# An 8-expert gated layer on rows sorted by expert, and two layer norms in one pass

## The chip, the core and the metric

The kernel runs on one core of one Trainium2 chip. It is one launch. The metric is the device time of that launch in microseconds, median over runs. The engines are TensorE (PE, its weight loads are PEld), VectorE (DVE), ScalarE (ACT), GpSimd (POOL) and the queue of SyncE (SP), which issues most DMAs; GpSimd issues the indirect ones, whose row numbers come from a table in on-chip memory.

## What is computed

Eight residual layers on x, four sequences of 512 tokens with 128 features: four times an attention and then a feed-forward layer, each on the layer norm of x and scaled by the tanh of a gate. The change touches two of them, the third attention (over latents) and the third feed-forward layer:

```
# third attention: its queries come from the norm of a norm
x = x + tanh(g_xattn[2]) * attn(ctx_1024, layernorm(x), ...)
  # inside: xn = ln(ctx) * g + b;  ln = ln(latents) * g' + b'

# third feed-forward: T = 2048 tokens, D = 128, F = 352, E = 8, TOP_K = 2
scores = softmax(xt @ router_w)
expert_weights, expert_idx = top_k(scores, 2)
h = gelu(xt @ w1[e]) * (xt @ v1[e])          # for every e
y = h @ w2[e]
out = sum over the two chosen e of weight * y  +  bias
x = x + tanh(g_ffn[2]) * out
```

The reference computes all eight experts for each token and keeps two.

## The kernel before

x is held transposed on chip (`c.xT`, features on the 128 partitions, 2048 tokens along the row), its layer norm in `c.xn`. The stages follow one another; each is one or several blocks, and between two blocks all engines meet at a barrier.

A layer norm (`layer_norm`) takes a list of pieces of at most 512 columns. For each piece TensorE multiplies by a centring matrix, ScalarE squares, TensorE averages the squares, ScalarE takes the logarithm of variance plus eps and the exponential of minus a half of it, VectorE multiplies. The third attention (`perceiver_attention`) calls it twice in two blocks: `norm_x` writes the norm of x to `c.xn` (4 pieces), and a second call norms `c.xn` once more in place (4 pieces) and the context (1 piece of 308 columns).

The third feed-forward layer (`dense_glu_moe`) starts with `norm_x` and `route`, which gives each token its two best experts (`top`, `place`). `expert_weights` spreads them over a table of eight weights per token, on VectorE. The main block is a loop over the 4 sequences; in each it goes through 24 units, three blocks of hidden features (128, 128 and 96) for each of 8 experts, in an order written by hand: `HP` and `VP` (hidden features on the partitions, 512 tokens along the row), then `YP` of the unit before, four products of 128 tokens. ScalarE takes the gelu (`gl`), VectorE multiplies it by `VP` (`hv`) and adds the finished expert, weighted, into `acc`. At the end of a sequence `acc` is turned back, scaled, and added to x. All 8 experts are computed for all tokens.

An earlier stage, the second feed-forward layer (`capacity_moe`, 64 experts, 3 per token), already works on sorted rows, and its rows in the trace are the nearest there are for the new code. It ranks tokens by matrix products with a triangular matrix, makes two tables of row numbers (`slot_in`, `slot_out`), and runs 32 pairs of experts. Each pair fetches 128 rows by an indirect DMA (`xs`), turns them (`XT`), multiplies (`HN`), turns the result (`HP`), multiplies again (`YP`), and scatters 128 rows to DRAM by another indirect DMA. At the end all rows are read back (`yg`), weighted (`acc`), turned and added to x.

## Time and profile before

| | |
|---|---|
| device time, median of 3 runs | 1845.82 us (1844.06 to 1846.3) |
| the profiled execution, device time | 1841.34 us |
| its span in the trace | 1839.5 us |
| mean granted clock of TensorE | 0.917 of full speed |
| PE busy | 1565.9 us, 85% |
| DVE, ACT, POOL busy | 847.9, 762.3, 432.8 us |

The profile is one execution, 4.5 us below the median of the runs. A busy TensorE row is not the same as TensorE at its peak, since matmuls overlap and their ends are modelled. In the rows further down, a stretch from A to B is in microseconds from the span's start, and PEclk is the clock that was granted to TensorE, 1.00 for 2.4 GHz and 0.50 for 1.2 GHz. The trace shortens tile names: `f_` stands for any feed-forward layer, so `f_W` is one of the weights W1 and W2, and `a_nx`, `a_nl` are the two norms of the third attention.

### The profile page before, as it was taken

The page shows a single profiled execution, that of the slowest core. Times are in us where ns is not written, and L with a number is a line of the kernel's source. Part 1 is how long each engine was busy: PE and PEld are TensorE (multiplying, and loading weights), DVE is VectorE, ACT ScalarE, POOL GpSimd, SP SyncE. Part 2 cuts the span into 40 slices and gives each one's busy share as a digit, 9 for nine tenths or more (in the row PEclk, how much of TensorE's full clock was granted, in tenths as well). Part 3 has the DMA queues.
Part 4 walks back from the last instruction along what each step waited for, and adds up shares of the span by engine and source line. Part 5 has one row for each costly group of instructions (what it writes and reads, how often), then busy time and mean ns, then how long its engine had stood idle before and what let it go on. Part 6 is the DMA issues. An engine that isn't in the chain of part 4 may idle for free. (4 is left out here: it accounts for less than half of the span.)

```text
span 1839.5 us, 21220 instructions
## 1 busy us (share of the span) xinstructions
PE 1565.9 (85%) x7428; PEld 694.9 (38%) x7428; DVE 847.9 (46%) x1637; ACT 762.3 (41%) x1379; POOL 432.8 (24%) x386
## 2 busy tenths in 40 slices
PE   6857778639946999999999999977999998776997
PEld 2223332325523333333333333324565564123443
DVE  5842278443333555455545545524343334524343
ACT  3443345334434656565655655541222224342111
POOL 1000062026401455455545445420000000100000
PEclk9978889759956999999999999997999999887999
DMA  8200030529240000000000000020000000000000
GB/s 279 92 12 0 26 81 1 191 80 345 100 122 1 1 1 1 1 1 1 1 1 1 1 0 1 1 98 1 1 0 0 0 0 29 1 30 27 0 0 23
DMA packets 32494, 71.27 MB, mean 39 GB/s; under 512 B 5747, under 2 KB 19827, under 8 KB 31375
## 3 DMA queue, kind: packets, MB, share of 16 engines
q1 hardware_dynamic: 30358, 65.93, 10.4%
q0 software_dynamic: 2048, 4.20, 0.8%
q8 instruction: 51, 0.84, 0.2%
q14 instruction: 37, 0.30, 0.1%
HBM read 65.92 MB, written 7.34 MB: 40 GB/s over the span
## 5 line engine op out<-in xcount | busy, mean ns | idle before, releaser
L1762 DVE TENSOR_REDUCE a_nmp<-a_SP 128x2 bf16<-128x590 f32 (+1 forms) x256 | 197.0, 769 | 267.5 <-PE a_SP L1531 265.6
L1690 ACT ACTIVATE a_prob<-a_TP 128x512 f32<-128x512 f32 x256 | 138.9, 595 | 154.8 <-PE a_TP L1519 153.7
L1549 PE MATMUL a_O<-a_prob,a_V 128*64 128x512 f32 (+1 forms) x640 | 172.2, 617 | 1.5 <-DVE a_on L1800 1.5
L1516 PE MATMUL a_TP<-a_qn,a_kn 64*128 64x512 f32 (+1 forms) x640 | 166.3, 597 | 1.0 <-DVE a_negm L1825 0.5
L1847 POOL TENSOR_TENSOR a_acc<-a_acc,a_prob 128x512 f32<-128x512 f32 x128 | 158.7, 1271 | 2.3 <-DVE a_acc L1813 1.6
L1245 DVE TENSOR_TENSOR f_hv<-f_gl,f_VP 128x512 f32<-128x512 f32 (+1 forms) x96 | 65.8, 686 | 163.5 <-ACT f_gl L1211 163.5
L1211 ACT ACTIVATE f_gl<-f_HP 128x512 f32<-128x512 f32 (+1 forms) x96 | 57.2, 595 | 200.7 <-PE f_VP L1193 200.7
L1837 POOL TENSOR_TENSOR a_acc<-a_prob 128x512 f32<-128x512 f32 x64 | 79.8, 1266 | 205.1 <-ACT a_prob L1690 205.1
L818 POOL TENSOR_TENSOR a_kxb<-a_kT,hmu 128x1232 bf16<-128x1232 f32 x9 | 21.7, 2409 | 414.4 <-DVE a_kxb L606 367.7
L1180 PEld LDWEIGHTS f_YP<-f_W,f_hv 128*128 128x128 f32 (+1 forms) x768 | 100.5, 192 | 47.9 <-issue 44.3
L1191 PE MATMUL f_HP<-xn,f_W 128*128 (+1 forms) x192 | 104.1, 625 | 16.4 <-PEq L1095 11.0
L1180 PE MATMUL f_YP<-f_W,f_hv 128*128 128x128 f32 (+1 forms) x768 | 101.7, 275 | 2.0 <-DVE f_hv L1245 2.0
L1193 PE MATMUL f_VP<-xn,f_V 128*128 (+1 forms) x192 | 101.7, 612 | 0.0
L665 DVE TENSOR_REDUCE a_nm<-a_SP 128x6 bf16<-128x462 f32 x144 | 78.3, 579 | 39.9 <-PE a_SP L365 24.4
L1531 PEld LDWEIGHTS a_SP<-a_knb,a_qnb 64*128 64x128 bf16 x512 | 24.8, 93 | 163.3 <-issue 86.7
L1531 PE MATMUL a_SP<-a_knb,a_qnb 64*128 64x295 bf16 (+1 forms) x512 | 76.5, 295 | 3.2 <-DVE a_nmp L1762 2.6
L827 POOL TENSOR_TENSOR a_biasQk<-a_biasQ,a_negQ 128x1232 bf16<-128x1232 f32 x12 | 32.4, 2710 | 198.1 <-DVE a_negQ L723 180.7
L1359 ACT ACTIVATE f_sl<-f_GP 128x512 f32<-128x512 f32 x40 | 23.9, 597 | 116.5 <-PE f_BP L1346 100.6
L1366 DVE TENSOR_TENSOR f_hu<-f_sl,f_UP 128x512 f32<-128x512 f32 x40 | 27.5, 688 | 81.3 <-ACT f_sl L1359 81.3
L365 PE MATMUL a_SP<-a_kxb,a_qb 128*128 128x462 bf16 x144 | 50.6, 374 | 15.3 <-DVE a_nm L665 9.7
L1519 PE MATMUL a_TP<-a_negm,a_sel 64*128 64x512 bf16 (+1 forms) x320 | 60.8, 376 | 0.0
L1516 PEld LDWEIGHTS a_TP<-a_qn,a_kn 64*128 64x128 f32 (+1 forms) x640 | 48.4, 181 | 30.0 <-DVE a_negm L1825 23.4
(377 smaller groups left out, 2776.6 us busy)
## 6 DMA issues: line engine op xcount, KB each, us to landing
ring_w<-in_F_w SPq DMA_DIRECT2D x64, 512.0 KB, 8.3
f_yg<-dispatched SPq DMA_DIRECT2D x12, 256.0 KB, 5.3
a_maskT<-in_maskT SPq DMA_DIRECT2D x4, 576.0 KB
a_biasT<-in_biasT SPq DMA_DIRECT2D x1, 2304.0 KB
f_b<-in_F_b SPq DMA_DIRECT2D x1, 1664.0 KB, 8.5
f_W<-in_F_w SPq DMA_DIRECT2D x1, 1536.0 KB, 11.9
f_W<-in_F_w SPq DMA_DIRECT2D x1, 1408.0 KB, 6.2
f_V<-in_F_v SPq DMA_DIRECT2D x1, 1408.0 KB, 9.1
```

What stands on the lines that cost most here:

```text
L665: nc.vector.tensor_reduce(nm[:, b % 2, qt, :].rearrange("p (g h) -> p g h", g=QUAD)[:, qs, hs], SP[:, slot_of[("unit", k)] % 2, 0:hi - lo] ...
L1180: mm = nc.tensor.matmul(YP[:, e % 2, q * P:(q + 1) * P], hv[0:wide(j), u % 3, q * P:(q + 1) * P], W2[0:wide(j), u, :], start=(j == 0 and q ...
L1191: nc.tensor.matmul(HP[0:wide(j), u % 2, :], W1[:, at:at + wide(j)], c.xn[:, tokens(b)], start=True, stop=True)
L1193: nc.tensor.matmul(VP[0:wide(j), u % 2, :], V1[:, at:at + wide(j)], c.xn[:, tokens(b)], start=True, stop=True).then_inc(hv_ready, 1)
L1245: nc.vector.tensor_tensor(hv[0:f, u % 3, :], gl[0:f, u % 2, :], VP[0:f, u % 2, :], ALU.mult).then_inc(multiplied, 1)
L1516: nc.tensor.matmul(TP[0:hi - lo, h, :], kn[HALF[h], g % 4, lo:hi], qn[HALF[h], g % 4, :], start=True, stop=False)
L1531: mm = nc.tensor.matmul(SP[:, h, 0:hi - lo], qnb[HALF[h], g % 2, q * P:(q + 1) * P], knb[HALF[h], g % 2, lo:hi], start=True, stop=True)
L1549: mm = nc.tensor.matmul(O[HALF[h], :], V[0:n, g % 4, kc, HALF[h]], prob[0:n, kc, h, :], start=kc == 0, stop=kc == NC - 1)
L1690: nc.scalar.activation(prob[0:n, kc, h, :], TP[0:n, h, :], ACT.Exp, bias=rowneg[0:n, g // NP:g // NP + 1] if kc == 0 else 0.0)\
L1762: nc.vector.tensor_reduce(nmp[:, u // 2, u % 2, :], SP[:, :, 0:hi - lo], AX.X, ALU.max, negate=True).then_inc(s_used, 1)
L1837: nc.gpsimd.tensor_tensor(acc[:, g % 2, h, :], prob[:, 1, h, :], prob[:, 2, h, :], ALU.add).then_inc(summed, 1)
L1847: nc.gpsimd.tensor_tensor(acc[:, g % 2, h, :], acc[:, g % 2, h, :], prob[:, kc, h, :], ALU.add).then_inc(summed, 1)
```

## The change

**Norms.** The third attention calls `layer_norm` once, with the context first and then the four pieces of x, reading `c.xT`. For the norm of a norm it uses that the variance of the first result is known: pieces named in `twice` take the logarithm of (1 + eps) times the variance plus eps squared.

**Experts.** `expert_weights` and the loop over all experts go. Each token now makes two rows, one for each chosen expert, and the 4096 rows are sorted by expert; every expert's part is filled up to a multiple of 128, so there are at most 39 tiles of 128 rows, each of one expert. A new block makes the tables on VectorE and TensorE and writes the normed rows to DRAM. The main block is written out for the 39 tiles, with one indirect fetch and one indirect scatter for each on GpSimd, and with the products the other way round: tokens on the partitions, 352 hidden features along the row, so that `hv` has to be turned (`HT`) before the last product. Which columns of W1, V1 and W2 a tile uses is read into a register of TensorE (`value_load`). The bias is added to x by one VectorE instruction at the start of the block. The end is the code of the second feed-forward layer, now the function `add_rows`, with two rows per token in place of three.

Diff, cut to its core:

```diff
@@ layer_norm
-                    nc.scalar.activation(lnv[:, i % 2, :w], var[:, i % 4, :w], ACT.Ln, bias=eps).then_inc(logged, 1)
+                    grow, add = (1.0 + eps, eps * eps) if i in twice else (1.0, eps)
+                    nc.scalar.activation(lnv[:, i % 2, :w], var[:, i % 4, :w], ACT.Ln, bias=add,
+                                         scale=grow).then_inc(logged, 1)
@@ perceiver_attention
-        norm_x(c, name + "_nx", start_loads)
-        layer_norm(c, name + "_nl", [(c.xn[:, s:s + S], c.xn[:, s:s + S], S) for s in range(0, T, S)]
-                   + [(c.ctxrep[:, :, 0:SK], cn[:, :], B * SK)])
+        layer_norm(c, name + "_n", [(c.ctxrep[:, :, 0:SK], cn[:, :], B * SK)]
+                   + [(c.xT[:, s:s + S], c.xn[:, s:s + S], S) for s in range(0, T, S)], start_loads, twice=(1, 2, 3, 4))
@@ dense_glu_moe, the table block (VectorE, for each of the two choices k)
+                    for k in range(TOPK):
+                        step(nc.vector.tensor_tensor(prod[:, :, :], hot[:, k, :, :], at[:, :, :], ALU.mult))
+                        step(nc.vector.tensor_reduce(pos[:, k, :], prod[:, :, :], AX.X, ALU.add))
+                        step(nc.vector.tensor_tensor(hit[:, k, :, :], per_tile(pos[:, k, :], HITS),
+                                                     over_tiles(bounds[:, :], HITS), ALU.is_ge))
+                        nc.vector.tensor_tensor(ids[:, k, :, 0:NT], hit[:, k, :, 0:NT], hit[:, k, :, 1:HITS],
+                                                ALU.subtract).then_inc(chosen, 1)
+                        step(nc.vector.tensor_reduce(full[:, k, :], hit[:, k, :, 1:HITS], AX.X, ALU.add))
...
+                        nc.vector.tensor_tensor(ranks[:, k, :, :], over_tiles(lanes[:, :], P),
+                                                per_tile(within[:, k, :], P), ALU.is_equal).then_inc(ranked, 1)
...
+                @block.gpsimd
+                def _(pool):
+                    for g in range(G):
+                        pool.wait_ge(stored[g], 16)
+                    pool.wait_ge(slot_in_made, 1)
+                    for n in range(FIRST):
+                        fetch(n)
@@ dense_glu_moe, the main block (FIRST = 2, XR = 8, YR = BEHIND = 4, WARM = 4, NT = 39)
+                for n in range(FIRST, XR):
+                    fetch(n)
+                for n in range(NT):
+                    if n + XR < NT:
+                        pool.wait_ge(rows_turned, n + 1)
+                        fetch(n + XR)
+                    if n >= BEHIND:
+                        scatter(n - BEHIND)
...
+                def up(n):
+                    pe.wait_ge(buf_ready, n + 1)
+                    if n >= 2:
+                        pe.wait_ge(multiplied, n - 1)
+                    columns = bass.ds(expert[n] * F, F)
+                    nc.tensor.matmul(HP[:, n % 2, 0:F], bufT[:, n % BR, :], W1[:, columns], start=True,
+                                     stop=True).then_inc(h_ready, 1)
+                    nc.tensor.matmul(VP[:, n % 2, 0:F], bufT[:, n % BR, :], V1[:, columns], start=True,
+                                     stop=True).then_inc(v_ready, 1)
+
+                def hidden(n):
+                    pe.wait_ge(multiplied, n + 1)
+                    if n:
+                        pe.wait_ge(h_copied, n)
+                    for j in range(NJ):
+                        mm = nc.tensor.transpose(HT[0:wide(j), j * P:(j + 1) * P], hv[:, n % 2, j * P:j * P + wide(j)],
+                                                 c.ident[:, :])
+                    mm.then_inc(h_turned, 1)
+
+                def down(n):
+                    pe.wait_ge(h_copied, n + 1)
+                    if n:
+                        pe.wait_ge(y_kept, n)
+                    for j in range(NJ):
+                        mm = nc.tensor.matmul(YP[:, 0:D], hT[0:wide(j), n % 2, j, :],
+                                              W2[0:wide(j), bass.ds(expert[n] * (NJ * P) + j * P, P)],
+                                              start=(j == 0), stop=(j == NJ - 1))
+                    mm.then_inc(y_ready, 1)
...
+                expert[0] = pe.value_load(expert_of[0:1, 0:1], min_val=0, max_val=E - 1)
+                for _ in range(WARM):
+                    nc.tensor.matmul(HP[:, 1, :], c.center[:, :], c.xn[:, 0:512], start=True, stop=True)
+                turn(0)
+                turn(1)
+                for n in range(NT):
+                    up(n)
+                    if n + 1 < NT:
+                        expert[n + 1] = pe.value_load(expert_of[0:1, n + 1:n + 2], min_val=0, max_val=E - 1)
+                    if n + 2 < NT:
+                        turn(n + 2)
+                    if n:
+                        hidden(n - 1)
+                    if n >= 2:
+                        down(n - 2)
...
+                for n in range(NT):
+                    act.wait_ge(h_ready, n + 1)
+                    if n >= 2:
+                        act.wait_ge(multiplied, n - 1)
+                    nc.scalar.activation(gl[:, n % 2, :], HP[:, n % 2, 0:F], ACT.Gelu).then_inc(gelued, 1)
+                    if n + 2 < NT:
+                        evacuate(n + 2)
+                    if n:
+                        copy_hidden(n - 1)
```

TensorE in the main block before, from the start of a sequence: `HP` and `VP` are products of 512 tokens with a block of W1 or V1, `YP` stands for four products of 128 tokens.

```order
L1191 MATMUL f2_HP<-xn,f2_W1 128x512
L1193 MATMUL f2_VP<-xn,f2_V1 128x512
L1178 ISA
L1180 MATMUL f2_YP<-f2_W2,f2_hv 128x128 x4
L1191 MATMUL f2_HP<-xn,f2_W1 96x512
L1193 MATMUL f2_VP<-xn,f2_V1 96x512
L1178 REGISTER_ALU
L1180 MATMUL f2_YP<-f2_W2,f2_hv 128x128 x4
```

TensorE in the main block now, one tile: `XT` turns the rows of the tile after next, `HT` turns the hidden rows of the tile before, `YP` is the last product of the tile before that.

```order
L1478 MATMUL f2_HP<-f2_W1,f2_bufT 128x352
L1480 REGISTER_ALU
L1480 MATMUL f2_VP<-f2_V1,f2_bufT 128x352
L1512 TENSOR_LOAD f2_expert_of
L1512 ISA x2
L1471 MATMUL f2_XT<-ident,f2_xs 128x128
L1488 MATMUL f2_HT<-ident,f2_hv 128x128
L1488 MATMUL f2_HT<-ident,f2_hv 128x128
L1488 MATMUL f2_HT<-ident,f2_hv 96x128
L1497 ISA
L1497 MATMUL f2_YP<-f2_W2,f2_hT 128x128
L1497 ISA
```

Three `YP` products stand in each tile. A load of a register with two instructions that check it stands between the last big product and the transposes, and instructions that compute an address stand before the products that use it.

VectorE between the router and the main block before, where `f2r_hot` marks the chosen experts:

```order
L1106 MEMSET f2r_wt 128x2048
L1114 TENSOR_TENSOR f2r_hot<-iota,f2r_place 128x128
L1116 TENSOR_TENSOR f2r_hot<-f2r_hot,f2r_top 128x128
L1114 TENSOR_TENSOR f2r_hot<-iota,f2r_place 128x128
L1116 TENSOR_TENSOR f2r_hot<-f2r_hot,f2r_top 128x128
L1117 TENSOR_TENSOR f2r_wt<-f2r_hot 128x16x8
```

The same place now, from the second choice on, where `f2_ids` and `f2_ranks` are the operands of the products `IX` that give the tables (the first of these rows up to `f2_ids<-f2_ids,iota` stand for the first choice as well):

```order
L1336 TENSOR_TENSOR f2_prod<-f2_hot,f2_at 128x128
L1337 TENSOR_REDUCE f2_pos<-f2_prod 128x16
L1338 TENSOR_TENSOR f2_hit<-f2_pos,f2_bounds 128x640
L1340 TENSOR_TENSOR f2_ids<-f2_hit 128x16x39
L1342 TENSOR_REDUCE f2_full<-f2_hit 128x16
L1343 SCALAR_TENSOR_TENSOR f2_within<-f2_full,f2_pos 128x16
L1345 TENSOR_TENSOR f2_ranks<-f2_lanes,f2_within 128x2048
L1348 TENSOR_TENSOR f2_ids<-f2_ids,iota 128x16x39
L1350 TENSOR_TENSOR f2_begun<-iota,f2_base 128x312
L1353 TENSOR_REDUCE f2_te<-f2_begun 128x39
L1354 TENSOR_SCALAR f2_te<-f2_te 128x39
L1355 CAST f2_expert_of<-f2_te 128x39
```

VectorE's part between router and main block grows from 6 instructions to 52. GpSimd, which had nothing in this stage, gets 78 indirect DMAs.

## Rows read from the trace of the kernel before

**Rows 1.** Stretches: busy time of each engine (instructions), PEclk, DMA share, GB/s.
```profile
1251.00:1255.30 4.30, 0.01 (x1) 0.01 (x1) 3.38 (x8) 0.37 (x1) 0.00 (x0) 0.50 0.00 0
1255.30:1534.70 279.40, 264.10 (x1168) 161.63 (x1169) 102.79 (x232) 61.19 (x102) 0.00 (x0) 0.96 0.00 0
364.80:403.60 38.80, 10.20 (x144) 8.87 (x144) 22.68 (x45) 16.91 (x61) 7.76 (x8) 0.50 0.17 44
403.60:503.90 100.30, 98.39 (x810) 54.25 (x810) 31.15 (x99) 42.21 (x97) 52.80 (x55) 0.98 0.61 224
503.90:532.30 28.40, 4.46 (x16) 2.87 (x16) 11.51 (x37) 5.12 (x16) 1.70 (x2) 0.55 0.44 118
532.30:545.30 13.00, 9.90 (x16) 3.78 (x16) 2.77 (x4) 8.29 (x14) 0.00 (x0) 0.76 0.52 184
545.30:559.50 14.20, 11.28 (x20) 4.68 (x20) 3.24 (x5) 9.34 (x17) 0.00 (x0) 0.80 0.00 1
```

**Rows 2.** Timeline, one unit of the all-expert loop: start, us, engine, line, operation.
```profile
1382.16 1.02 PE L1193 MATMUL f_VP<-xn,f_V 128*128 x2
...
1383.02 1.06 PE L1180 MATMUL f_YP<-f_W,f_hv 96*128 96x128 f32 x8
...
1383.22 0.60 ACT L1211 ACTIVATE f_gl<-f_HP 128x512 f32<-128x512 f32 x1 [2.02 <-PE f_VP L1193]
...
1383.85 0.69 DVE L1245 TENSOR_TENSOR f_hv<-f_gl,f_VP 128x512 f32<-128x512 f32 x1 [1.93 <-ACT f_gl L1211]
...
1383.91 1.02 PE L1191 MATMUL f_HP<-xn,f_W 128*128 x2
```

**Rows 3.** Timeline, one pair in the second feed-forward layer's loop.
```profile
450.03 1.08 PE L2155 MATMUL f_HN<-ring_w,f_bufT 128*64 128x512 f32 x4
...
451.04 0.33 PE L2147 MATMUL f_XT<-ident,f_xs 128*128 128x128 f32 x1
...
451.30 1.09 PE L2175 MATMUL f_YP<-ring_w,f_hg 128*64 128x128 f32 x16
...
451.37 0.98 POOL L2125 DMA_INDIRECT dispatched<-f_ys,f_slot_out  x1 [0.62 <-DVE f_ys L2216]
...
452.33 0.66 PE L2164 MATMUL f_HP<-ident,f_hn 128*128 128x128 f32 x4
...
452.66 0.97 POOL L1945 DMA_INDIRECT f_xs<-token_rows,f_slot_in  x1 [0.30 <-issue]
...
452.91 1.08 PE L2155 MATMUL f_HN<-ring_w,f_bufT 128*64 128x512 f32 x4
```

**Rows 4.** Timeline, making of the tables and start of the loops.
```profile
1252.85 0.29 DVE L1114 TENSOR_TENSOR f2r_hot<-iota,f2r_place 128x128 f32<-128x128 f32 x1
...
378.95 1.22 DVE L2014 TENSOR_TENSOR f_ranks<-iota,f_pos 128x1024 bf16<-128x1024 f32 x1
...
390.44 0.18 DVE L2024 CAST f_slot_in<-f_row 128x32 uint32<-128x32 f32 x1
...
391.51 1.15 POOL L1945 DMA_INDIRECT f_xs<-token_rows,f_slot_in  x1 [93.93 <-DVE f_slot_in L2024]
...
400.47 0.94 POOL L1945 DMA_INDIRECT f_xs<-token_rows,f_slot_in  x1 [0.30 <-issue]
...
403.67 6.56 PE L2182 MATMUL f_HP<-xn,center 128*128 128x512 f32 x10 [14.57 <-PEq L1970]
...
410.78 1.08 PE L2155 MATMUL f_HN<-ring_w,f_bufT 128*64 128x512 f32 x4 [0.34 <-ACT f_bufT L2242]
```

**Rows 5.** Timeline, the end of the second feed-forward layer.
```profile
503.77 0.29 DVE L2216 TENSOR_TENSOR f_ys<-f_YP,f_b 128x128 f32<-128x128 f32 x1 [1.29 <-PE f_YP L2175]
...
504.93 0.97 POOL L2125 DMA_INDIRECT dispatched<-f_ys,f_slot_out  x1 [0.30 <-issue]
...
512.30 9.01 SPq L2277 DMA_DIRECT2D f_yg<-dispatched  x12
...
518.18 2.20 DVE L2306 SCALAR_TENSOR_TENSOR f_acc<-f_yg,f_gk,f_acc 128x128 f32<-128x128 f32 x8 [14.11 <-ACT f_acc L2286]
```

More of the change, by code:

```diff
@@ L127, in _, with layer_norm @@
             dve.wait_ge(got, 8)
-def layer_norm(c, name, pieces, loads=None, scratch=None, eps=LN_EPS):
+def layer_norm(c, name, pieces, loads=None, scratch=None, eps=LN_EPS, twice=()):
     nc = c.nc
@@ L1123, in dense_glu_moe @@
     nc, d = c.nc, c.dram
-    E, F = 8, 352
+    E, F, TOPK, G = 8, 352, 2, 4
     NJ = -(-F // P)
-    U = E * NJ
-    with ExitStack() as ctx, c.phase():
+    NT = (T * TOPK + E * (P - 1)) // P
+    HITS, PAD = NT + 1, 8
+    XR, BR, YR, BEHIND, FIRST, WARM = 8, 4, 4, 4, 2, 4
+    ROWS_AT = 5120
+    xrows = nc.dram_tensor("glu_rows", [T, D], F32, kind="Internal").ap()
+    with ExitStack() as whole, ExitStack() as ctx, c.phase():
+        gk = whole.enter_context(nc.sbuf_tensor(name + "_gk", [P, TOPK, TILES], F32))
         router = Router(c, ctx, name + "r", E, "F2_router")
@@ L1145, in dense_glu_moe @@
[L1145 to L1151 removed]
         def wide(j):
             return min(P, F - j * P)
+        W1, V1 = sb("W1", [P, E * F]), sb("V1", [P, E * F])
@@ new lines, in dense_glu_moe, with _, scatter @@
+        h_turned, h_part, h_copied, y_ready, y_kept, bias_made, biased = (
+            sem(n) for n in ("h_turned", "h_part", "h_copied", "y_ready", "y_kept", "bias_made", "biased"))
+        scattered = [sem(f"scattered{i}") for i in range(YR)]
+        with nc.Block() as block:
+            @block.gpsimd
+            def _(pool):
+                def scatter(n):
+                    pool.wait_ge(y_kept, n + 1)
+                    nc.gpsimd.indirect_dma_start(
+                        out=c.disp[:, :], out_offset=bass.IndirectOffsetOnAxis(ap=slot_out[:, n:n + 1], axis=0),
+                        in_=ys[:, n % YR, :], in_offset=None).then_inc(scattered[n % YR], 16)
+                for n in range(FIRST, XR):
[6 more added lines that the diff above has]
+                        scatter(n - BEHIND)
+                for n in range(NT - BEHIND, NT):
+                    scatter(n)
+                for i in range(YR):
+                    pool.wait_ge(scattered[i], 16 * len(range(i, NT, YR)))
@@ L1216, in _, with keep @@
+                copy_hidden(NT - 1)
+                act.wait_ge(h_part, NT)
             @block.vector
             def _(dve):
-                dve.wait_ge(loaded, 64)
+                def keep(n):
+                    dve.wait_ge(y_ready, n + 1)
+                    if n >= YR:
+                        dve.wait_ge(scattered[n % YR], 16 * (n // YR))
+                    nc.vector.tensor_copy(ys[:, n % YR, :], YP[:, 0:D]).then_inc(y_kept, 1)
+                dve.wait_ge(w_loaded, 64)
                 nc.vector.tensor_tensor(bias[:, 1:2], bias[:, 0:1], c.gates[:, gate:gate + 1],
@@ L1253, in _ @@
-                dve.wait_ge(x_updated, B)
+                dve.wait_ge(bias_made, 1)
+                nc.vector.tensor_scalar(c.xT[:, :], c.xT[:, :], bias[:, 1:2], None, ALU.add).then_inc(biased, 1)
+                for n in range(NT):
+                    dve.wait_ge(gelued, n + 1)
+                    dve.wait_ge(v_ready, n + 1)
+                    if n >= 2:
+                        dve.wait_ge(h_turned, n - 1)
+                    nc.vector.tensor_tensor(hv[:, n % 2, :], gl[:, n % 2, :], VP[:, n % 2, 0:F],
+                                            ALU.mult).then_inc(multiplied, 1)
+                    if n >= 2:
+                        keep(n - 2)
@@ L1256, in shared_moe @@
+                keep(NT - 2)
+                keep(NT - 1)
+                dve.wait_ge(biased, 1)
+        ctx.close()
+        add_rows(c, name, gate, ROWS_AT, TOPK, gk)
 def shared_moe(c, name, gate):
@@ L2326, in flamingo_kernel @@
+        add_rows(c, name, gate, 4096, TOPK, gk)
 def flamingo_kernel(nc, dram, out):
```

414 lines of the change are left out of this document (270 added, 144 removed).

## The prediction

> **What bounds the kernel now.** First the page's busy shares: TensorE is the busiest engine by far, so a stage is worth what TensorE's row in it is worth. Then the busy time by stretches [rows 1]. The loop over all experts takes 279.4 us, and TensorE is busy for 264.1 of them at a granted clock of 0.96. It is bound by its matmuls. Then the timeline of one unit [rows 2]: `VP` starts at 1382.16, `YP` at 1383.02 and the next `HP` at 1383.91, with no gap between them, while ScalarE and VectorE work 0.60 and 0.69 us of each 2.6. For the new code I read the second feed-forward layer, which has the same kind of loop: its tables take 38.8 us, its loop 100.3 us with TensorE busy for 98.4, its end 28.4 us [rows 1]. Last the two norms of the third attention, 13.0 and 14.2 us [rows 1].
>
> **The main loop: the price of a tile.** From rows 2, a product of 512 columns takes 0.86 us and eight passes of 128 columns 0.89 with the change to the next product, 0.107 a pass (a product in f32 is two passes). So `HP` and `VP` of 352 columns cost 2 x 0.86 x 352/512 = 1.18 us. The three last products are six passes of 128 columns, 0.65. Four transposes (one of fetched rows, three of `hv`) cost 0.58, as the four do between 452.33 and 452.91 [rows 3]. Changing kind costs something: in rows 3 the parts alone would be 0.86 + 0.14 + 0.86 + 0.58 = 2.44, and a pair takes 452.91 - 450.03 = 2.88, so 0.44 for three changes, 0.15 each. Here there are two such changes and one like the 0.03 of rows 2. Sum 1.18 + 0.65 + 0.58 + 0.33 = 2.74 us.
>
> Who else could pace a tile? GpSimd: a scatter starts at 451.37 and the fetch behind it at 452.66 [rows 3], 1.29 us, 1.27 without the difference of the two, so one of each is 2.56 us. That is below 2.74, but close. ScalarE: a gelu and three copies, none over the 0.60 of rows 2, under 2.0 us. VectorE: a product of 352 columns (0.53, between the 0.29 for 128 and the 0.69 for 512) and a copy (0.29). The buffers: `HT`, `YP` and `XT` are single. `copy_hidden(n-1)` ends about 2.7 us into tile n (up 1.18, turn and three transposes to 1.9, two copies), and the next transposes need it at 2.74 + 1.5. `keep` is done 0.5 us into the next tile and is needed at 1.9. No wait ends last there.
>
> **The register load** is what the trace of before doesn't show. Its lower bound is 0: the last wait ahead of it that comes late is for `y_kept`, 0.5 us into the tile before, and what is queued by then and behind it (three transposes' rest, the last products, the next `HP` and `VP`) keeps TensorE busy until 2.74 + 1.18 = 3.9 us. A load of up to 2 us is covered, if the sequencer may run that far ahead. The upper bound is that the load starts only when the products have ended, so nothing covers it. The nearest row is another engine that picks up a fresh number and starts: from `slot_in` written at 390.62 to GpSimd's first DMA at 391.51, 0.89 us [rows 4]. With the check and the address instructions I put the upper end at 1.2 us. I take 0 in the loop, because the wait ahead of it ends early enough, and 1.0 once at the start, where nothing covers it.
> The Trainium skill (DMA: Bandwidth & Descriptors, section Latency and other measured facts) gives a floor of about 600 ns for a `tensor_load`; no row here shows one. Uncovered in each of 39 tiles it would be an estimate of 23 us, and the forecast would be 1740. The same skill (TensorE: Matmul & The Clock Gate, section Architectural detail: the array is 16× 32×32, not 1× 128×128) says that TensorE's queue is 64 deep, by which the load would be covered; rows 2 agree as far as they go, since `YP` follows `VP` without a gap though a wait stands between them.
>
> **The tables.** VectorE's instructions cost 0.16 us plus 1.04 ns per element of a row: 0.29 for 128, 1.22 for 1024 [rows 4]. Ahead of the two choices stand 20 small ones, 4.9 us, with some 14 waits on the one before at 0.035, together 5.4. Each choice has 128, 128, 640, 624, 624, 16, 2048 and 624 elements: 0.29 + 0.29 + 0.83 + 0.81 + 0.81 + 0.18 + 2.29 + 0.81 = 6.3, with waits 6.5, twice 13.0. The experts of the tiles cost 1.5 (312 elements twice, two small ones). The products `IX` of the second choice run beside these. Then four instructions to `slot_in`, 1.2. Sum 21.1 us. From the start of the `slot_in` instruction to the first warming product it is 403.67 - 390.44 = 13.23 us with eight fetches [rows 4]; six fetches fewer at (400.47 - 391.51)/7 = 1.28 leave 5.5. Together 21.1 - 0.2 + 5.5 = 26.4 us from the start of the block at 1251.0. From there to the first `up` 410.78 - 403.67 = 7.1 [rows 4], less one warming product (0.86), plus the first load (1.0): 7.3. The other six fetches and the addition of the bias (2048 elements, 2.3 us on VectorE) lie beside the warming. If the table block's rates are off by a fifth, it is 4 us either way.
>
> **The end.** From the start of the last `up` the chain is: products 1.18, `hv` to 1.9, the transposes queue behind the tile before to 3.3, two copies to 4.25, last product to 5.0, `keep` to 5.5 us. What follows is the 28.4 us of the layer before (503.9 to 532.3, rows 1), with these differences: the last row is kept at 504.06 there (-0.15), and two scatters stand behind it, one here (-0.6, the last one starts at 504.93, rows 5). Twelve reads are issued in 9.01 us [rows 5], eight in 6.0 (-3.0), and the last group has four additions in place of eight at 2.20 us (-1.1). That leaves 23.5.
>
> **The sum for this stage.** After 1251.0: 26.4 + 7.3 + 38 x 2.74 (104.1) + 5.5 + 23.5 = 166.8 us. Before: 4.3 + 279.4 = 283.7 [rows 1]. A gain of 116.9. The next stage's norm then starts at a colder clock: the end of the other layer shows 0.55, and the norm behind it 13.0 us at 0.76 [rows 1]. Before, TensorE came to it from a dense loop. I take 1.1 of this, between 0 and 2.4. Gain 115.8.
>
> **The norms.** The first block of 13.0 us goes, and the second stays as it is in size: one piece of 308 and four of 512 columns, 14.2 us [rows 1]. Its clock was 0.80 and will be nearer to the 0.76 of the block that started behind `add_rows`, some tenths of a microsecond. The weight loads of this attention now start with the block that stays; they take most of the first one (DMA share 0.52 of 13.0 us, rows 1, some 7 us of transfer), so they end inside 14.2. The cover is 5 us or more; gone, they would cost what sticks out. The extra scale in the logarithm is free, since the instruction has one already. Gain 12.8, between 11.5 and 13.5.
>
> **Total.** 128.6 us. The profiled execution of 1841.3 us becomes 1712.7; it stood 4.5 us below the median of the runs, so 1717 against 1845.8.
>
> **The rivals.**
> B, the load isn't covered. A tile costs 2.74 plus 0.5 to 1.2 us. For it: this stage has many short instructions between products (a load, two checks, an addition, three addresses), and in rows 3 there are none. Against it: the wait ahead ends early. At 0.9 it is 39 x 0.9 = 35 us, 1752; at the upper end 47, 1764.
> C, GpSimd paces the tiles. If changes between kinds cost less than 0.15, TensorE goes below 2.56 and GpSimd's two DMAs are the bound: 38 x 0.18 = 7 us less, 1710. In rows 3 it waited 0.62 of 2.88 us for VectorE, so it is near. Its other side, DMAs that take longer with more rows in flight, is against rows 1: the loop there ran with a DMA share of 0.61, here no weights are loaded beside it.
> D, slower than before. The holes of B could make the granted clock fall to 0.50 (1.2 GHz) for the whole loop, as in the table stretch, where TensorE is busy 10.2 of 38.8 us [rows 1]. Then the 2.74 doubles and the load adds 1.2: 6.7 us a tile, 38 x 3.9 = 150 us more, 1867. It decides from 2.74 + 129/38 = 6.1 us a tile on. Against it: TensorE would still be busy for more than half of each tile, and the norm block behind a hole, busy for 9.90 of 13.0 us, got back to 0.76.
> E, the norms don't gain what they should, because the loads are late: at most 7 us, 1724. It lies inside the forecast's own range.
> That the change doesn't do what it says can't be for the tiles, since their number is fixed at 39.
>
> **How the numbers follow.** The forecast (load covered, 2.6 to 2.9 us a tile, tables within 4 us) has 0.58 and its own range is 1708 to 1728. B has 0.28, C 0.10, D 0.02, and 0.02 is left for sizes of several terms off at once, up to 1800. The range of 8 in 10 runs from 1704 (C with a quicker table block) to 1763 (nearly all of B). A measurement tells 0.2%, 3.7 us, from no change; all cases but D and the rest lie far below, so faster 0.97, same 0.01, slower 0.02.
>
> **What would show it.** In the profile after: the starts of successive `HP` 2.7 to 2.8 us apart, with TensorE busy over 90% of the loop and a clock near 0.98 (B: 3.2 to 4.0 and a hole behind `VP`; C: 2.56 with TensorE waiting for `XT`'s rows); the table block 26 us from its first instruction to the first warming product; the stage's end 23 us; one norm block of 14 us in the third attention. Wrong would be above all a hole of a microsecond between `VP` and `XT` in every tile, or a clock of 0.5 in the loop.

## The result, and the profile after

The changed kernel takes 1696.54 us (median of 4 runs, 1692.21 to 1698.05) against 1846.03 (4 runs, 1844.06 to 1846.3). The ratio is 0.9189, 95% interval 0.917 to 0.9207: 149.5 us less, where 128.8 were forecast. The time lies 7.5 us below the stated range, 1704 to 1763. The profiled executions, 1697.39 and 1841.34 us, are 144.0 apart (spans 1695.6 and 1839.5).

The same kind of view as [rows 1], of the kernel after: tables, warming, loop, end of the layer, the next norm, and the one norm block that the third attention has left.

```profile
1237.00:1262.94 25.94, 7.57 (x51) 6.10 (x52) 20.83 (x54) 5.27 (x8) 2.38 (x3) 0.50 0.16 46
1262.94:1269.50 6.56, 6.11 (x10) 2.51 (x11) 0.47 (x1) 0.50 (x2) 5.08 (x5) 0.66 0.19 40
1269.50:1358.12 88.62, 85.87 (x517) 67.29 (x517) 29.83 (x73) 47.39 (x150) 65.46 (x67) 1.00 0.19 51
1358.12:1388.33 30.21, 9.29 (x47) 6.43 (x45) 8.92 (x25) 6.84 (x23) 3.88 (x4) 0.64 0.30 81
1388.33:1401.40 13.07, 9.98 (x16) 3.79 (x16) 2.77 (x4) 8.29 (x13) 0.00 (x0) 0.76 0.30 100
532.00:546.20 14.20, 10.81 (x20) 4.77 (x20) 3.25 (x5) 9.61 (x16) 0.00 (x0) 0.83 0.48 168
```

Every stretch but one is within 1.3 us of the forecast. The loop is not: its 38 steps take 88.6 us where 104.1 were predicted. The timeline of a tile, to set beside [rows 2, 3]:

```profile
1318.35 0.76 PE L1478 MATMUL f_HP<-f_W,f_bufT 128*128 x2
1318.94 0.75 PE L1480 MATMUL f_VP<-f_V,f_bufT 128*128 x2
1319.48 0.97 POOL L1239 DMA_INDIRECT f_xs<-glu_rows,f_slot_in  x1 [0.30 <-issue]
1319.53 0.27 PE L1471 MATMUL f_XT<-ident,f_xs 128*128 128x128 f32 x1
1319.64 0.49 PE L1488 MATMUL f_HT<-ident,f_hv 128*128 128x128 f32 x3
1319.97 0.83 PE L1497 MATMUL f_YP<-f_W,f_hT 128*128 x6
1320.64 0.76 PE L1478 MATMUL f_HP<-f_W,f_bufT 128*128 x2
```

Start to start: 0.59 for `HP`, 0.59 for `VP`, 0.11 for `XT`, 0.33 for the three `HT`, 0.67 for `YP`, 2.29 in all. No step from one kind of product to the next costs anything that can be read here, and the register load between `VP` and `XT` leaves no hole. The granted clock of the loop is 1.00. The whole loop averages 2.33: in five tiles from 1320 us on VectorE waits for a scatter to land, and in two of these TensorE waits for VectorE, 1.1 and 1.7 us. Its third wait of the kind, 0.6 us, is in the last tile and not behind a scatter. The waits of this stretch (engine, line, releaser: us in total, times, longest), and one such place:

```profile
DVE f_ys L1561 <- DMA dispatched<-f_ys,f_slot_out: 8.9, 5, 3.3
PE f_YP L1497 <- DVE f_ys L1561: 3.3, 3, 1.7
```

```profile
1329.83 0.29 DVE L1561 COPY f_ys<-f_YP 128x128 f32<-128x128 f32 x1 [2.64 <-DMA dispatched<-f_ys,f_slot_out]
1330.04 0.51 DVE L1573 TENSOR_TENSOR f_hv<-f_gl,f_VP 128x352 f32<-128x352 f32 x1
1330.37 0.93 PE L1497 MATMUL f_YP<-f_W,f_hT 128*128 x6 [1.07 <-DVE f_ys L1561]
```

The register load is on TensorE's sequencer, the part that issues its instructions (PEldq; line, operation, count, ns least/median/most, first and last start). The load itself takes 0.30 us, half of the floor that the prediction quoted for it:

```profile
L1512 PEldq TENSOR_LOAD <-f_expert_of x38: 296/302/414, 1269.6 to 1355.1; - x38
L1512 PEldq FUSED_REGOPS  x38: 151/151/156, 1270.0 to 1355.5; - x38
L1512 PEldq SEQ_ASSERT  x38: 18/18/18, 1270.3 to 1355.7; - x38
```

### The profile page after: what moved, and what is told of

Same layout as the page of the kernel before. It is cut to its first block and busy times, and to the rows that moved or that the text cites. A ratio compares the mean times of both kernels' runs of the same rounds, so it can differ in the third digit from the quotient of the medians.

```text
span 1695.6 us, 20327 instructions
## 1 busy us (share of the span) xinstructions
PE 1401.8 (83%) x6865; PEld 612.3 (36%) x6865; DVE 799.9 (47%) x1546; ACT 753.6 (44%) x1445; POOL 510.1 (30%) x464
## 5 line engine op out<-in xcount | busy, mean ns | idle before, releaser
L2273 POOL DMA_INDIRECT f_xs<-token_rows,f_slot_in x32 | 31.0, 968 | 113.7 <-DVE f_slot_in L2352 93.9
L1239 POOL DMA_INDIRECT f_xs<-glu_rows,f_slot_in x39 | 38.4, 984 | 71.8 <-DVE f_slot_in L1361 58.0
L417 PE MATMUL a_TP<-a_qT,a_kx 32*103 32x512 f32 (+1 forms) x288 | 42.2, 656 | 19.8 <-DVE a_added L709 7.1
L2018 ACT ACTIVATE a_prob<-a_TP,a_rowneg 77x512 f32<-77x512 f32 x64 | 40.3, 680 | 39.4 <-PE a_TP L1847 39.4
L2530 DVE TENSOR_TENSOR f_hb<-f_HP,f_b 128x256 f32<-128x256 f32 x64 | 24.2, 420 | 67.5 <-PE f_HP L2492 67.5
L2190 POOL TENSOR_TENSOR a_knb<-a_kn,a_onesf 128x294 bf16<-128x294 f32 x32 | 21.7, 678 | 106.4 <-DVE a_kn L2095 106.4
```

The lines of the kernel that those rows point to most:

```text
L417: nc.tensor.matmul(TP[0:r, g, :], kx[row, b, i * CR:i * CR + r], qT[row, tokens(b)], start=True, stop=False, tile_position=(32 * g, 0))
L1239: nc.gpsimd.indirect_dma_start(out=xs[:, n % XR, :], out_offset=None, in_=xrows[:, :], in_offset=bass.IndirectOffsetOnAxis(ap=slot_in[:, n ...
L2018: nc.scalar.activation(prob[0:n, kc, h, :], TP[0:n, h, :], ACT.Exp, bias=rowneg[0:n, g // NP:g // NP + 1] if kc == 0 else 0.0)\
```

## The experiments

Theories. **S**: in rows 3 the 0.44 us beyond the parts are four changes between weight tiles of 64 and of 128 columns, 0.11 to 0.15 each; the new loop has tiles of 128 only. **K**: every change of kind costs 0.15, as predicted. **I**: the sequencer issues that pair's many instructions too slowly. And **L**: GpSimd's 2.57 us for a fetch and a scatter do not pace a tile of 2.29 only because it has a lead.

Loops are compared by the starts of ScalarE's first and last gelu, one to a tile, which every trace has in full. The changed kernel's loop takes 88.6 us in its first trace, and 86.7 and 88.5 in those of two repeats (`after_again`, `after_fourth`); 38 tiles of 2.29 would be 87.0, and the first two and the last are shorter. So a difference of 2 us between two loops is within what one kernel shows. Each ratio is to the kernel before on the same chip, with its 95% interval.

**The two parts, each alone, and the changed kernel again.** In `norms_only` the third attention calls the one pass and the feed-forward layer is the old one; in `experts_only` it is the other way round:

```diff
-        layer_norm(c, name + "_n", [(c.ctxrep[:, :, 0:SK], cn[:, :], B * SK)] ..., twice=(1, 2, 3, 4))
+        norm_x(c, name + "_nx", start_loads)
+        layer_norm(c, name + "_nl", [(c.xn[:, s:s + S], c.xn[:, s:s + S], S) for s in range(0, T, S)] ...)
```

> The kernel before with the two norms of the third attention made in one pass, and the old loop over all experts. Step tested: the norms' gain of 12.8 us. If the traces are read rightly, the first of the two norm blocks (13.0 us) goes and the one that stays is as long as it was, so 12.9 us less than before, 1833 against 1846, with the first product of the latent attention 12.9 us after where it would be with one block less. Rival (the weight loads stick out once the expert layer behind them is the old one): a gain of 6 to 11 us. Both parts must add up: this gain and that of the kernel with the expert layer alone should give the 149.5 us of both within 3 us.

> The changed kernel with the old two norms. Step tested: what the layer on sorted rows gives by itself. By the two traces the stage goes from 306.5 to 174.1 us (132.4 less), and the block behind it and the rest of the kernel give back 2.5, so 130 us less span than before; with the two norms behind it instead of one, the clock is back sooner for the products and the give-back may be 1 us less. Expected 1710 to 1716. If instead the 4.5 us by which the profiled execution of before lay under its median is a property of the program of before (its loop), the medians show 4 to 6 us more gain here than the traces do (135 us, 1711) and none in the kernel with the norms alone.

> The changed kernel once more, unaltered, as the yardstick of this chip. 149 us less than before, 1697. Sum of the two parts 143 us by the traces' terms (12.9 + 130). If the sum of the parts' medians is also 143 to 146, the remaining 4 to 6 us are between the profiled execution of before and its median, and in no part of the kernel.

Beside 1843.51 for the kernel before (11 runs), `norms_only` took 1829.7 (ratio 0.9929, 0.9916 to 0.9942), `experts_only` 1707.83 (0.9266, 0.9251 to 0.9282) and `after_again` 1696.91 (0.9207, 0.9192 to 0.9222). So the parts gain 13.8 and 135.7 us, together 149.5, against 146.6 for both at once, just within the 3 us allowed. The norms are worth what was forecast (12.8) or a little more: from the first norm's start to the first product `a_PRA` it was 32.5 us before, and is 19.5 in `norms_only` (532.22 to 551.69) and 19.7 in the kernel after. `experts_only` came out below the 1710 to 1716 expected, at 1708, with the loop at 87.0 us (first gelu 1281.35, last 1368.32). The test of the 4.5 us did not decide: the sum of the parts is above the 143 to 146 expected, but the unaltered kernel gained 2.9 us less here than at first.

**Tiles of 64 columns.** On `fixed_columns` (below), `HP` and `VP` made in halves:

```diff
-                    nc.tensor.matmul(HP[:, n % 2, 0:F], bufT[:, n % BR, :], W1[:, columns], start=True,
-                                     stop=True).then_inc(h_ready, 1)
...
+                    for out, w, ready in ((HP, W1, h_ready), (VP, V1, v_ready)):
+                        for h in (0, 64):
+                            mm = nc.tensor.matmul(out[h:h + 64, n % 2, 0:F], bufT[:, n % BR, h:h + 64], w[:, columns],
+                                                  start=True, stop=True)
+                        mm.then_inc(ready, 1)
```

> The changed kernel with each of the two products up made as two halves of 64 rows (weight tiles of 64 columns, as the products of the second feed-forward layer have them), and the expert of a tile fixed at n // 5 by the program, so that the columns are not those of the tile's own expert. In the second feed-forward layer a pair takes 2.88 us where its parts sum to 2.44; in the changed loop a tile takes 2.29 and its parts sum to nothing more. Theory S (the 0.44 us are changes between weight tiles of 64 and of 128 columns, 0.15 or more each): here two such changes per tile, so 2.29 + 0.3 to 0.4 = 2.6 to 2.7 us a tile, the loop 9 to 15 us longer than the 88.7 of the changed kernel (part of it covered by the waits for GpSimd), and the profile shows the extra ahead of VP's successor and ahead of HP. Theory K (every change of kind of product costs 0.15, and the new loop hides it somehow) and theory I (the sequencer of TensorE issues the 28 instructions of such a pair too slowly): K gives 2.29, no change; I gives at most what six more instructions cost, under 0.15 us a tile. If two halves do not run side by side the products up double, 1.18 us a tile, 45 us.

The kernel took 1703.19 us (0.9236, 0.9219 to 0.9253). TensorE's timeline of a tile, again by starts:

```profile
1302.50 0.81 PE L1480 MATMUL f_HP<-f_W,f_bufT 128*64 128x352 f32 x4
1303.14 0.76 PE L1480 MATMUL f_VP<-f_V,f_bufT 128*64 128x352 f32 x4
1303.83 0.33 PE L1471 MATMUL f_XT<-ident,f_xs 128*128 128x128 f32 x1
1304.00 0.49 PE L1489 MATMUL f_HT<-ident,f_hv 128*128 128x128 f32 x3
1304.32 0.83 PE L1498 MATMUL f_YP<-f_W,f_hT 128*128 128x128 f32 x6
1305.09 0.81 PE L1480 MATMUL f_HP<-f_W,f_bufT 128*64 128x352 f32 x4
```

A tile takes 2.59, 0.30 more, the same in every tile behind the first two, and the loop 96.7 us: 8 more than the first trace after, a little under the 9 to 15 expected, since TensorE's waits of that trace are gone here. `VP` to `XT` grew from 0.59 to 0.69 and `YP` to `HP` from 0.67 to 0.77, the two changes of width; `HP` and `XT` grew by 0.05 each. Two halves run side by side, so it is not the columns. K is refuted, since its changes of kind are in both kernels and cost nothing in one. S has its size, and set back into [rows 3] it fits each of the four steps there. By starts they take 1.01, 0.26, 1.03 and 0.58 us, and the products alone 0.86, 0.11, 0.86 and 4 x 0.107 = 0.43; the differences are 0.15, 0.15, 0.17 and 0.15. I is not what decides: this kernel has no register load, and the sequencer's 1.09 us of other issue work, worked out below, lies 1.5 under the tile, far more than the few added products need.

The rows of the weight loads (PEld) show where the time goes. Here is the one for `XT`, first in the pair of [rows 3], between two widths, then in the changed kernel's tile above:

```profile
451.04 0.14 PEld L2147 LDWEIGHTS f_XT<-ident,f_xs 128*128 128x128 f32 x1 [0.81 <-issue]
...
1319.24 0.14 PEld L1471 LDWEIGHTS f_XT<-ident,f_xs 128*128 128x128 f32 x1
```

The first starts together with its product (451.04), the second 0.29 us ahead of it (1319.53), beside `VP`. In `halves` the load for `XT` again starts with its product (1303.83), and so does the one for `HP` (1305.09), which the changed kernel starts 0.11 ahead (1318.24 and 1318.35). At a change of width the load of the next weights is not covered by the product before.

The Trainium skill (TensorEngine Tiling (Array Packing), section Key Properties) says that changing the tiling mode drains TensorE, and changing the tile alone does not. By that rule the forecast would have had no such term in a loop of one width; the traces agree with it, 0.15 us a change with what stands around it.

**The register load: none, two, five.**

```diff
-                        expert[n + 1] = pe.value_load(expert_of[0:1, n + 1:n + 2], min_val=0, max_val=E - 1)
+                        expert[n + 1] = (n + 1) // 5
```

and with `for _ in range(5):` or `range(2)` ahead of the load.

> The changed kernel without the register load: the program fixes the expert of tile n as n // 5, so that the weight columns of a tile are not those of its own expert. It prices the load as it stands. If it is covered (this case's reading: 0.3 us for the load and some 0.17 for what follows it, on TensorE's sequencer, in a tile of 2.29 us with TensorE busy throughout), the tile stays at 2.29 us, the loop at 86.7 to 88.7 us (first gelu to last), and only the load ahead of the warming products goes, 0 to 1 us: 1694 to 1698. Rival (a part sticks out in each tile): the tile falls by 0.05 us or more, the loop by 2 us and up to 0.47 x 39 = 18 us.

> The changed kernel with each tile's register load made five times over, 4 x 38 loads more. It asks how large the cover is. By the changed kernel's trace one load and its reading cost the sequencer 0.3 to 0.47 us, so five take 1.5 to 2.35 us. If the sequencer runs ahead of the matmuls by less than a tile and has some 1 us of other issue work per tile, the cover ends: the tile becomes 2.5 to 3.4 us and the loop 8 to 42 us longer than 86.7, with a hole in TensorE's row behind VP. If all five stay covered (the sequencer's other work under 0.7 us a tile), the tile stays 2.29.

> Two register loads per tile, once more. By 1.09 + 0.65 per load the sequencer needs 2.39 a tile. In the last call, whose stretches behind GpSimd's last fetch are the only even ones, a tile took 2.45 with two loads beside 2.29 with one. Expected now without late releases: 2.39 to 2.45 throughout, the loop from first gelu to last 91 to 93.5 us beside 86.7 to 88.6, 3 to 6 us slower than the changed kernel. Rival (each further load costs its whole 0.65): 20 to 25 us slower.

Without a load: 1693.89 (0.9199, 0.9185 to 0.9213), within the interval of the changed kernel. A tile is 2.29, so the load costs nothing there; ahead of the warming products TensorE is idle for 6.4 us instead of 7.3, so the first load costs 0.9 (1.0 in the prediction). The loop takes 89.9 us and not the 86.7 to 88.7 expected, because VectorE waits for 13 scatters, 21.3 us in all, and TensorE for VectorE behind them. Five: 1770.01 (0.962, 0.9602 to 0.9638), 4.34 us a tile where nothing else waits, the loop 165.0, which is 76 to 78 us more, where I held 42 for the most. Two: 1701.98 (0.9227, 0.9211 to 0.9243), 2.46 a tile, the loop 92.2, as expected. In the trace with five, the idle time behind `VP` and the even tile:

```profile
1301.59 0.75 PE L1480 MATMUL f_VP<-f_V,f_bufT 128*128 x2
1304.18 0.30 PE L1471 MATMUL f_XT<-ident,f_xs 128*128 128x128 f32 x1 [1.84 <-issue]
...
1305.93 0.75 PE L1480 MATMUL f_VP<-f_V,f_bufT 128*128 x2
```

Its loads start 0.65 us apart (1300.8 to 1303.4), the next tile's first at 1305.2. That leaves 4.34 - 5 x 0.65 = 1.09 us a tile for the sequencer's other work. By this sum it needs 1.74, 2.39 and 4.34 us for one, two and five loads, and a tile takes the larger of this and 2.29. The 1.09 is fitted to five loads; two loads are its test, and their 2.46 is 0.07 over it. By the same sum the load of the changed kernel is covered with some 0.55 us to spare. That the sequencer runs ahead is in the trace itself: up to 1301.4 it has started 16 loads, and the sixteenth stands in the program behind the sixteenth `VP`, which runs at 1302.90.

**GpSimd's lead.**

```diff
-    XR, BR, YR, BEHIND, FIRST, WARM = 8, 4, 4, 4, 2, 4
+    XR, BR, YR, BEHIND, FIRST, WARM = 8, 4, 8, 4, 2, 4      (deep)
+    XR, BR, YR, BEHIND, FIRST, WARM = 4, 4, 4, 4, 2, 4      (shallow)
```

> The changed kernel with eight buffers for kept rows (ys) in place of four. In its trace VectorE waits for a scatter to land in some tiles from 1320 us on (some 9 us in five waits, by which TensorE loses 2 to 3.3 us in three places), since GpSimd issues 76 transfers at 1.285 us, 97.7 us, beside 88.7 us of tiles. With eight buffers those waits go: tile 2.29 throughout, loop 86.7 to 87.2 us. But GpSimd's last scatter can't be issued before 1262.5 + 97.7 = 1360.2 + what it waited, and the last tile's rows are kept at 1361 at the earliest, so the end stays within a microsecond of where it is: 0 to 2 us less. Rival (GpSimd is no bound at all): the full 2 to 3.3 us less. Rival (nothing: the two waits are paid back by the end): 0.

> The changed kernel with four buffers for fetched rows (xs) in place of eight, so that GpSimd's lead is four tiles shorter: it fetches two tiles beside the warming products instead of six, and each later fetch waits for a tile four back. Theory L (GpSimd's 2.57 us for a fetch and a scatter are no pace of the tiles in the changed kernel only because of its lead of eight fetches and four kept rows): here the tile is 2.57 us in the stretch in which every tile has a fetch and a scatter (tiles 4 to 34), with TensorE waiting for xs, and the loop is 6 to 9 us longer, 93 to 96 us. Rival (its two transfers overlap somehow with each other, so that 2.57 is never a bound): 2.29 a tile and no change.

`deep`: 1695.72 (0.9206, 0.9194 to 0.9219); no wait for a scatter is left, all tiles behind the first two are 2.29, the loop is 85.3 us. That is 1.4 to 3.3 less than the changed kernel's; whether any of it reaches the median is within the noise. `shallow`: 1698.33 (0.9223, 0.9209 to 0.9237), an interval that overlaps that of the changed kernel, the loop 88.7 where 93 to 96 were expected. My 2.57 a tile from tile 4 on was wrong: the first 27 tiles still take 2.29, then some wait for fetched rows (TensorE 2.3 us in all, in three waits). GpSimd falls behind by 2.57 - 2.29 = 0.28 a tile, and a lead of four tiles, 9 us, is used up only near the thirtieth. So L holds in kind, since the waits come late and at the buffer that was made short, and the lead that 38 tiles take is 38 x 0.28 = 10.6 us. Its price in time is not shown: the loop of 88.7 lies in the range of the changed kernel's own.

**No warming products** (WARM = 0), and this with YR = 8, beside the changed kernel:

> The changed kernel unaltered, as the yardstick of the three beside it. On the chip of the last call it took 1722 us, and in its trace ScalarE and VectorE are released 1 to 4 us late, over and over, in this loop (107.3 us in place of 86.7) and in the second feed-forward layer (119.8 from first fetch to last scatter in place of 113.4), while GpSimd issues its transfers. If that belongs to that chip, it is 1697 again on another one, with 149 us less than before, and no late releases. If it belongs to the kernel's state in some executions, late releases are seen again here.

> No warming products, once more. As before: 5.9 us of warming go, the first two or three tiles run at the lower clock and give back 2 to 4 us; 0 to 2 us less than the changed kernel. Rival (the clock stays low): 5 us or more slower.

> Eight buffers for kept rows and no warming products, once more: 2 to 5 us less than the changed kernel if the loop without late releases is bound by its products and GpSimd has some 4 us in hand; 0 to 2 if GpSimd's 76 transfers set the end.

The changed kernel took 1698.2 (0.9203, 0.9186 to 0.922), without warming products 1692.77 (0.9174, 0.9158 to 0.9191), and with the deeper buffers too 1688.06 us (0.9153, 0.9139 to 0.9167). The last, `deep_nowarm_again`, is 10 us below the changed one, where 2 to 5 were expected; the middle one is 5.4 below, where 0 to 2 were. The start of the last:

```profile
1263.64 0.47 PE L1471 MATMUL f_XT<-ident,f_xs 128*128 128x128 f32 x1 [7.24 <-issue]
1264.79 1.42 PE L1478 MATMUL f_HP<-f_W,f_bufT 128*128 x2
1266.00 1.38 PE L1480 MATMUL f_VP<-f_V,f_bufT 128*128 x2
1267.93 0.47 PE L1471 MATMUL f_XT<-ident,f_xs 128*128 128x128 f32 x1 [0.55 <-DMA f_xs<-glu_rows,f_slot_in]
1268.20 0.81 PE L1478 MATMUL f_HP<-f_W,f_bufT 128*128 x2
```

Only the first tile's products run at 1.2 GHz (1.21 us to the next start instead of 0.59), the second tile's already at 2.4; its stretches 1262 to 1270 and 1270 to 1280:

```profile
1262.00:1270.00 8.00, 5.37 (x16) 3.11 (x17) 2.26 (x4) 3.26 (x7) 5.47 (x5) 0.61 0.15 35
1270.00:1280.00 10.00, 10.00 (x61) 7.78 (x60) 3.47 (x9) 5.75 (x20) 7.62 (x8) 1.00 0.23 52
```

The first gelu comes 2.6 us behind the first transpose instead of 7.5 behind the first warming product, and the loop is 86.8. Then GpSimd sets the end, as the rival had it: its 76 transfers (the starts of the first and the last) run from 1263.22 to 1359.74 without a gap, 1.287 us each, the last scatter 6.7 us behind the last gelu instead of 5.2. The stage takes 169.3 us instead of 173.9, so 4.6 less. Of the spans' difference of 10.2 us, 1.3 more lie ahead of the stage and 4.3 behind it, where the two kernels have the same code. Those behind lie in the next norm block and the 17 us after (first the changed kernel, then this one; a stretch of 13 us from the start of the norm, then 17):

```profile
1390.34:1403.34 13.00, 10.08 (x16) 3.84 (x16) 2.77 (x4) 8.27 (x13) 0.00 (x0) 0.76 0.32 100
1403.34:1420.34 17.00, 16.72 (x52) 9.12 (x52) 12.34 (x28) 7.91 (x14) 2.66 (x2) 0.82 0.00 0
```

```profile
1384.45:1397.45 13.00, 9.93 (x20) 4.19 (x21) 3.25 (x5) 9.20 (x14) 0.00 (x0) 0.87 0.33 100
1397.45:1414.45 17.00, 14.73 (x54) 7.48 (x52) 15.76 (x35) 8.61 (x16) 2.89 (x2) 1.00 0.01 2
```

The same block at the same place in the program, at 0.87 instead of 0.76, then 1.00 instead of 0.82: the granted clock rose earlier behind the hole. Why, the runs do not show, and it isn't tied to this edit: kernels with the warming products have it too, `fixed_columns` and `loads5` at 0.85 and `after_again` at 0.83, each then at 1.00. From the start of that norm to the end, with the same code, the changed kernel takes 307.2, 303.7 and 306.1 us in its three traces, `loads5` 302.0 and `deep_nowarm_again` 301.8. So the trace gives 4.6 us to the edit and leaves the rest of the 10 open. The 4.6 are also more than the 0 to 2 that I expected in case GpSimd sets the end: in the changed kernel the same 76 transfers run from 1264.54 to 1366.13, 101.6 us instead of 96.5, so GpSimd itself lost 5 us there to waits for VectorE. Without the deeper buffers VectorE waits 32.5 us for landings instead of 9.6, the loop is 93.8 us, and the stage is no shorter (174.8); but this trace is of an execution 4.4 us above its median. Whether the missing warming products gain anything by themselves is not shown: the two ratios' intervals overlap at their ends.

**A chip on which both kernels are slower.** The same kernels also ran on another chip, where the kernel before took 1849.88 us:

> The changed kernel unaltered, as the yardstick for the three kernels beside it. 1697 us, 149 less than before.

> The changed kernel with each tile's register load made twice. In the kernel with five loads per tile TensorE's sequencer starts them 0.65 us apart, and from the transpose behind the last one (1304.15) to the next tile's first load (1305.2) 1.05 us pass, together 4.34 a tile. If the sequencer is the pace only from there on, a tile costs the larger of 2.29 and 1.05 to 1.09 + 0.65 per load: one load 1.74, covered with 0.55 to spare; two loads 2.39, so 0.10 us a tile and 4 us in the loop more than the 85.3 without waits, about 89 (beside the changed kernel's 86.7 to 88.6, whose waits for GpSimd it partly takes in): 1697 to 1701. Rival (the hole of five loads comes from the queue behind the load running empty in another way, so that each load over the first costs its whole 0.5 to 0.65 us): tile 2.8 to 2.9, loop 20 to 25 us longer, 1720.

> The changed kernel without the four warming products before the loop. They take 5.87 us at a granted clock of 0.66 for the stretch. The first product up can then start some 5 us sooner, but the first tiles run at the lower clock (1.2 GHz in place of 2.4): if it rises after about as many busy microseconds as in the changed kernel (4 to 6), two or three tiles take 4.6 instead of 2.29, and 2 to 3 us of the 5 are left. GpSimd's 74 remaining transfers then have 5 us less of a lead, and its waits in the loop (1 to 3 us of TensorE) grow by 1 to 3. Expected 0 to 2 us less than the changed kernel. Rival (the clock stays low for longer because short products with waits between them do not raise it): 5 us or more slower.

> Eight buffers for kept rows and no warming products. With the eight buffers alone the loop has no waits left (38 tiles in 85.3 us) and GpSimd waits for TensorE 1.2 us a tile at the end, so it has some 4 us in hand. Then the 2 to 3 us of the missing warming products come through: 2 to 5 us less than the changed kernel, 1692 to 1695. Rival (GpSimd's 76 transfers of 1.285 us from 1262.5 on are the bound, 1360.2 at the earliest for the last scatter beside 1364.2 in the changed kernel): at most 4 us less, of which the waits for its landings take 1 to 2.

They took 1722.52 (0.932, 0.9306 to 0.9333), 1722.6 (0.9317), 1722.26 (0.9302) and 1719.36 (0.9292), in the order of these texts. The changed kernel gains 127 us there instead of 149, so the four times test none of their own steps; eight buffers without warming products are 3.2 us below the changed kernel. The waits of the changed kernel's loop there name a releaser, "remote", that no trace from another chip has:

```profile
ACT f_hT L1535 <- remote: 13.0, 7, 2.6
ACT f_gl L1547 <- remote: 9.1, 6, 2.4
DVE f_hv L1573 <- remote: 5.2, 2, 2.6
```

One place in that loop. The gelu is done at 1304.55 and the transpose at 1304.33, and both who wait for them start at 1305.5, a microsecond late and within 0.02 of each other:

```profile
1304.06 0.27 PE L1471 MATMUL f_XT<-ident,f_xs 128*128 128x128 f32 x1
1304.09 0.46 ACT L1547 ACTIVATE f_gl<-f_HP 128x352 f32<-128x352 f32 x1 [1.15 <-PE f_HP L1478]
...
1305.52 0.27 ACT L1529 COPY f_bufT<-f_XT 128x128 f32<-128x128 f32 x1 [0.97 <-PE f_XT L1471]
1305.54 0.52 DVE L1573 TENSOR_TENSOR f_hv<-f_gl,f_VP 128x352 f32<-128x352 f32 x1 [1.89 <-PE f_VP L1480]
```

The loop takes 107.3 us, with tiles of 2.0 to 4.7 while GpSimd fetches and scatters, and of 2.29 again once only scatters are left (from 1371 us on). The loop of the second feed-forward layer, which both kernels have, takes 119.8 us from its first fetch to its last scatter instead of 113.4. The median of the kernel before is 4 to 9 us above those on other chips, which these 6 us would explain; there is no trace of it from this chip, so that is not shown. The four traces from this chip have 18 to 31 such waits each, all other traces none. Two loads per tile took 2.45 in the even part.

## Why the prediction was wrong

**The tile's price** failed, in the sentence "Changing kind costs something: ... 0.44 for three changes, 0.15 each". The 0.44 was real, its cause wrong: it belongs to the changes of tile width, four in that pair and none in the new loop (`halves`). The same cost hid in the 0.58 for four transposes, which was read up to such a change; a transpose is 0.11. With both corrected the prediction's own terms give 1.18 + 0.65 + 0.43 + 0.03 = 2.29, to the hundredth. That is 38 x 0.45 = 17.1 us too much, of which the waits for GpSimd, less the shorter first and last tiles, gave 1.6 back.

**GpSimd as a floor** of 2.56 a tile failed too, inside rival C, which had the right direction for the right reason ("if changes between kinds cost less than 0.15"). It stopped at 1710 because a rate was taken for a bound per tile. GpSimd issues six fetches beside the warming products and ends with scatters alone; over the loop it was short by 10.6 us, and had most of that in hand.

**The offset** of 4.5 us between the profiled execution of before and its median was carried over to the kernel after. There the profiled execution stands 0.9 above it. That is 5.4 of the 20.7 us, and belongs to no step. It is of the size by which the gain itself varies: 149.5, 146.6 and 145.9 us in three comparisons of the same two kernels.

Right: the register load (0 in the loop, 0.9 at the start, and for the reason given, a sequencer that runs ahead), tables 25.9 (26.4), first warming product to first `up` 6.6 (7.3), the norms 12.9 in the trace (12.8), their weight loads covered, the next norm 13.1 at 0.76 where it was 11.9 at 0.88, so 1.2 (1.1) longer. This last one is in part luck: from 12.1 to 13.5 us were seen for that block in kernels with the same code there. From the last `up` to the next stage 30.2 us (5.5 + 23.5 = 29.0): the eight reads are issued in 5.30 us instead of 6.0, but they begin 9.07 us behind the last scatter's start, where it was 7.37 in [rows 5]:

```profile
1363.62 0.29 DVE L1561 COPY f_ys<-f_YP 128x128 f32<-128x128 f32 x1 [1.21 <-PE f_YP L1497]
1364.19 0.97 POOL L1446 DMA_INDIRECT dispatched<-f_ys,f_slot_out  x1 [0.54 <-DVE f_ys L1561]
1373.26 5.30 SPq L1023 DMA_DIRECT2D f_yg<-dispatched  x8
```

The sum by the traces: the layer from its norm to the next stage 306.5 before, 174.1 after, 132.4 less; norms 12.9, with 1.1 more gained ahead of the layer; 2.5 given back behind it (1.2 in the norm block, 1.3 after, at the colder clock). 143.9, the difference of the spans.

Rival B, given 0.28, is refuted for one load. From three loads a tile on it would have been the answer, by the sequencer's sum; that was not run. Rival D is refuted by the loop's clock of 1.00.

## What to carry to other kernels

When a residue is left between the parts of a measured loop and its period, list everything that alternates in it (kind of product, tile width, data type, accumulator) before a new loop is charged with it; here the tile column of the same rows, 128*64 beside 128*128, told it. An engine that is slower per step than the loop is a bound only once its deficit times the steps exceeds its lead, so count both. And ask what products placed only to raise the clock cost now that real products stand ready behind them.

## What the runs showed of the hardware

A register load from on-chip memory takes TensorE's sequencer 0.30 us, 0.65 with its checks and the gap to the next. One in a tile of 2.29 us was hidden, two made it 2.46 and five 4.34. A change between weight tiles of 64 and 128 columns cost 0.15 us with its surroundings, and there the load of the next weights started with its product and not ahead of it. GpSimd issued one indirect transfer of 128 rows every 1.29 us where it waited for no other engine. And on one chip ScalarE and VectorE were released late, by a microsecond and more, in the loops in which GpSimd issues transfers densely. The changed kernel is 25 us slower there than on the others, of which its two such loops show 18.7 and 6.4. What the late release is was not found.
